# Joining two experts' rows and the attention projection: where the second expert's rows are added

## The reference

```python
x = L0_attn_x
xn = _layernorm(x, axis=-1)
x = x + _L0_attn_ref(xn, Wq, Wk, Wv, Wo, bo) + _L0_ffn_ref(xn, router_logits, gating_einsum, linear, per_expert_scale, router_scale)
```

## Time and profile before

| | |
|---|---|
| median of three runs | 814.1 us |
| the profiled execution's own time | 815.55 us |
| its span, first to last instruction | 813.8 us |
| TensorE busy in the span | 94% |
| VectorE, ScalarE, GpSimd busy | 67%, 57%, 53% |
| mean rate of all transfers | 121 GB/s |
| last scatter landed | 781.55 us |
| from there to the end of the span | 32.3 us |

### The profile page before, as it was taken

One profiled execution on the slowest core, in us unless ns is written; L12 is line 12 of the kernel. 1 busy time (PEld: TensorE's weight loads), 2 busy tenths in 40 slices (PEclk: granted clock), 3 DMA queues, 4 the chain that ended last, 5 costly groups with the idle time before them and its releaser, 6 DMA issues.

```text
span 813.8 us, 17685 instructions
## 1 busy us (share of the span) xinstructions
PE 766.9 (94%) x6172; PEld 468.4 (58%) x6172; DVE 546.2 (67%) x1419; ACT 466.9 (57%) x984; POOL 433.7 (53%) x561
## 2 busy tenths in 40 slices
PE   8999999999999999999999999879899899998997
PEld 6555554444444434444444444328889789888976
DVE  5458879999999888888888888303344334433348
ACT  3564567777777677777777777774333333333310
POOL 7665542231324545655475453264686667666676
PEclk9999999999999999999999999999999999999999
DMA  8895562513233134243442350113533333322777
GB/s 202 250 296 175 171 190 57 157 34 91 81 93 99 40 96 131 61 103 106 107 98 66 95 158 16 36 41 88 155 104 111 111 105 111 104 84 83 235 247 240
DMA packets 74912, 98.20 MB, mean 121 GB/s; under 512 B 16588, under 2 KB 54092, under 8 KB 74764
## 3 DMA queue, kind: packets, MB, share of 16 engines
q1 hardware_dynamic: 65960, 78.34, 34.2%
q0 software_dynamic: 8864, 18.72, 7.4%
HBM read 63.53 MB, written 30.75 MB: 116 GB/s over the span
## 4 chain that ended last, share of the span: by engine, by line
PE 50%; POOL 13%; issue 12%; ACT 4%; DVE 3%; DMA 2%; another core or an unknown queue 1%; DVEq 0%; POOLq 0%; ACTq 0%
PE banks L1154 17%; PE banks L754 16%; PE banks L746 13%; POOL expert_rows L1243 7%; POOL stacks L593 5%; ACT probs L1092 4%; PE banks L1339 3%; DVE stacks L1438 2%; PE banks L1348 1%; DMA stacks<-xn_rows,places 1%; DVE junk L708 1%; PE banks L1269 0%; DMA w_gu<-expert_rows 0%; DMA expert_rows<-stacks,places 0%
## 5 line engine op out<-in xcount | busy, mean ns | idle before, releaser
L708 DVE CUSTOM_DVE_ANT_0 junk<-banks,mask 128x128 bf16<-128x128 f32 (+7 forms) x512 | 359.6, 753 | 55.7 <-issue 50.6
L1092 ACT ACTIVATE probs<-banks 128x512 f32<-128x512 f32 x576 | 310.7, 606 | 102.7 <-PE banks L754 98.4
L754 PE MATMUL banks<-stacks 105*128 105x512 bf16 (+3 forms) x768 | 199.4, 329 | 10.1 <-issue 5.4
L746 PE MATMUL banks<-stacks 102*128 102x512 bf16 (+3 forms) x768 | 172.6, 326 | 2.2 <-DVE maxima L708 2.0
L885 POOL TENSOR_SCALAR_AFFINE_SELECT probs<-probs 128x512 f32<-128x512 f32 x128 | 79.9, 643 | 103.3 <-ACT probs L1092 99.5
L1321 DVE TENSOR_TENSOR probs<-banks,probs 128x256 f32<-128x256 f32 x71 | 30.1, 423 | 150.6 <-ACT probs L1285 125.0
L754 PEld LDWEIGHTS banks<-stacks 105*128 105x128 bf16 x768 | 65.6, 97 | 103.5 <-ACT probs L1092 40.5
L1154 PE MATMUL banks<-probs,ctxT 128*17 128x256 f32 (+2 forms) x1920 | 114.4, 360 | 2.0 <-DVE banks L1073 1.1
L1243 POOL DMA_INDIRECT expert_rows<-stacks,places x71 | 79.9, 1126 | 62.4 <-ACT stacks L1290 48.1
L746 PEld LDWEIGHTS banks<-stacks 102*128 102x128 bf16 x768 | 69.1, 98 | 72.2 <-DVE maxima L708 17.5
L1285 ACT ACTIVATE probs<-banks 128x256 f32<-128x256 f32 x71 | 27.3, 385 | 109.7 <-PE banks L1339 66.4
(11 more groups left out here) (129 smaller groups left out, 781.2 us busy)
## 6 DMA issues: line engine op xcount, KB each, us to landing
stacks<-qk_parts SPq DMA_DIRECT2D x192, 128.0 KB, 3.1
qk_parts<-ctxT SPq DMA_DIRECT2D x32, 384.0 KB, 3.3
xn_rows<-probs SPq DMA_DIRECT2D x8, 512.0 KB, 5.1
ctxT<-inverse_sums SPq DMA_DIRECT2D x8, 512.0 KB
w_gu<-in_w_gu SPq DMA_DIRECT2D x8, 512.0 KB
stacks<-in_x SPq DMA_DIRECT2D x16, 256.0 KB
ctxT<-expert_rows SPq DMA_DIRECT2D x16, 256.0 KB, 3.6
w_gu<-expert_rows SPq DMA_DIRECT2D x16, 256.0 KB, 5.5
```

Of the source, the lines that this page charges most:

```text
L708: last = dve.tensor_tensor_reduce(junk[:, n % RING, c:c + w], mpsum[:, slot, c:c + w], keep["mask"][:, S - w:S], 1.0, 3 * NEG, ALU.add, AL ...
L746: last = pe.matmul(mpsum[:, slot, at + c:at + e], qs[hq][0:R_MAX, h, qt * P:(qt + 1) * P], ks[hq][0:R_MAX, h, c:e], start=True, stop=True)
L754: last = pe.matmul(score_bank(("S", n, h))[:, c:c + w], ks[hq][:, h, kt * P:(kt + 1) * P], qs[hq][:, h, q0:q0 + w], start=True, stop=True)
L1092: act.activation(probs[:, u % PRING, h], score_bank(("S", n, h)), ACT.Exp, scale=SCALE).then_inc(exp_done, 1)
```

## The change

The second expert's rows are no longer loaded into a buffer of their own. GpSimd issues, for each pair, a transfer from `expert_rows` whose destination is the buffer that holds the first expert's rows of that pair, with addition as the way of writing (`accum_op`): the DMA engines read the destination, add, and write it back. GpSimd's 16 additions and the buffer in `w_gu` are gone, so are SyncE's 16 loads and its two waits ahead of them. VectorE still makes two additions for a pair: the sum of the two experts' rows to the accumulator, and the product to it. The wait on `bias_set` goes from GpSimd's queue to VectorE's.

```diff
-    done_w = Room(keep["w_gu"][:, :, :].rearrange("p e h -> p (e h)"))
     halves = [Room(keep["ctxT"][:, 2 * m + 1]) for m in range(NP // 2)]
-    yk = [[halves[n // 2]([P, 2, D]) for n in range(NP)], [done_w([P, 2, D]) for _ in range(NP)]]
+    yk = [halves[n // 2]([P, 2, D]) for n in range(NP)]
...
-            load(0, n)
-        sp.wait_ge(before["y_free"], RR + NST)
-        sp.wait_ge(before["w_ready"], NST)
-        for n in range(NP):
-            load(1, n)
+            load(n)
...
     def on_gpsimd(pool):
-        pool.wait_ge(before["bias_set"], NP)
         for n in range(NP):
             pool.wait_ge(loaded[0][n], 16)
-            pool.tensor_tensor(flat(acc[:, 2 * n:2 * n + 2, :]), flat(acc[:, 2 * n:2 * n + 2, :]), flat(yk[0][n]), ALU.add).then_inc(first_ready, 1)
+            pool.dma_start(yk[n], y_rows[1][:, 2 * n:2 * n + 2, :], accum_op=ALU.add).then_inc(loaded[1][n], 16)
...
     def on_vector(dve):
+        dve.wait_ge(before["bias_set"], NP)
         for n in range(NP):
             rows = acc[:, 2 * n:2 * n + 2, :]
-            dve.wait_ge(first_ready, n + 1)
             dve.wait_ge(loaded[1][n], 16)
-            dve.tensor_tensor(flat(rows), flat(rows), flat(yk[1][n]), ALU.add).then_inc(second_ready, 1)
+            dve.tensor_tensor(flat(rows), flat(rows), flat(yk[n]), ALU.add).then_inc(second_ready, 1)
```

More of the change, by code:

```diff
@@ L1381, in combine @@
     out_done = sem("out_done")
-    proj_ready, first_ready, second_ready, pair_done = (sem(name) for name in ("proj_ready", "first_ready", "second_ready", "pair_done"))
+    proj_ready, second_ready, pair_done = (sem(name) for name in ("proj_ready", "second_ready", "pair_done"))
     flat = lambda a: a.rearrange("p t d -> p (t d)")
@@ L1387, in on_sync, with load @@
     def on_sync(sp):
-        def load(k, n):
-            sp.dma_start(yk[k][n], y_rows[k][:, 2 * n:2 * n + 2, :]).then_inc(loaded[k][n], 16)
+        def load(n):
+            sp.dma_start(yk[n], y_rows[0][:, 2 * n:2 * n + 2, :]).then_inc(loaded[0][n], 16)
         sp.wait_ge(before["scaled"], NP)
```

## The result

| | before | changed |
|---|---|---|
| median, same chip | 814.5 us (812.2 to 816.3, 6 runs) | 821.4 us (817.8 to 824.9, 6 runs) |
| ratio | | 1.0087, interval 1.0053 to 1.0121 |
| the profiled execution, and its span | 815.55, 813.8 us | 817.79, 815.9 us |
| issue behind the last scatter's landing | 781.61 | 776.92 |
| from there to the end of the span | 32.2 us | 39.0 us |

What follows compares the result with a forecast made beforehand. VectorE set the pace before; after the change, full DMA engines: from 782.9, 16 x 1.44 + 14 x 0.72 = 33.1 us, then 0.8, 1.4 and 2.57 give 820.8, plus 0.3: 821.1 us. Range 819 to 823; 8 in 10, 810.5 to 829.

Steps and rivals of the forecast that it cites:

- The bound: After the last scatter: full DMA engines, 1.44 us per adding transfer, 0.72 per store; VectorE and TensorE wait; chance 0.38.
- The sum: Last stage: movement of 33.1 us from 782.9, then 0.8, 1.4 and 2.57 us, ending the span at 820.8.
- First landing: GpSimd's first adding transfer, issued at 781.8, lands at about 784.5 to 785.2, at load speed.
- the rival in which TensorE decides: Last stage: second read free, 0.72 us a pair, TensorE's chain sets the end; 810.4 to 811.1; chance 0.23.
- the limit of 1.66 us a pair: Spacing of adding transfers' landings at which gain turns to loss; forecast wrong if they come closer together.
- What is removed: GpSimd's 16 additions, worth at most 5.9 us through VectorE; SyncE's 16 loads and the `bias_set` wait, worth nothing.
- 3.0 to 3.7 us: Most of the 5.9 us that can be had, since TensorE's pair 4 waits for VectorE's pair 0.
- Issue: GpSimd's queue: adding transfers issued 1.3 us apart, hidden by the 1.44 us of movement.
- The rival of 2.3 us a transfer: GpSimd's issue priced per row, transfers 2.3 us apart; time 824.1 us; chance 0.12.
- The free second read: DMA engines: destination read costs nothing, 0.72 us a pair, TensorE decides; 810.4 to 811.1; chance 0.23.
- A price by piece above the double: DMA engines: adding 1 KB rows costs more than double; at three times 832.6 us; chance 0.15.
- The half price: DMA engines: second read costs half, 1.08 us an adding transfer; time 815.4 us; chance 0.12.

Runs made afterwards that it cites:

- e_plain: Changed kernel with GpSimd's 16 transfers overwriting instead of adding; stretch 29.1 us, 0.9971 against the kernel before.
- e_late_stores: Changed kernel with SyncE's 16 stores begun only when all adding transfers have landed; stretch 40.2 us, 1.0102 against the kernel before.
- v_split4: Kernel before, with VectorE making the first-row additions of pairs 0 to 9 early, four matmul banks; stretch 28.7 us, ratio 0.9991.
- e_2k: Changed kernel with each adding transfer reading 128 runs of 2 KB instead of 256 of 1 KB; stretch 36.9 us, 1.0073 against the kernel before.
- e_half: Changed kernel with only even pairs by adding transfer, odd pairs loaded by SyncE and added by VectorE; stretch 35.3 us, 1.0075 against the kernel before.

## Why the prediction was right

The time was forecast as 821.1 us, and slower; the median is 821.4. That these agree to 0.3 us is more than the prediction can claim: the changed kernel's own runs lie 7 us apart. Nor is the step from span to time sound. It added 0.3 us, the median less the span of another execution, where an execution's own time is 815.55 - 813.8 = 1.75 us above its span before and 1.9 after; the forecast span of 820.8 stands against spans of 815.9 to 823.0 with a median of 819.5. What can be held to the prediction are its steps.

- **The bound.** Forecast, with a chance of 0.38: the DMA engines are full and everything waits for the landing of adding transfers, which cost them two moves each. Shown: e_plain takes the addition away and gives back 10 us of 39; e_late_stores measures 1.36 us by itself, where 1.44 had been taken, against 0.72 to 0.77 for a plain transfer in as many packets. The pace was 2.20 us against the 2.16 of the sum. That it is the second read that costs, and not another part of adding, was argued and is not shown.
- **The sum.** From the landing to the end 820.8 - 781.55 = 39.25 us were forecast; the two traces have 39.6 and 40.0. It came out so with terms that were off in opposite ways. The DMA engines began at about 778.9, 2.6 us behind the landing, where 782.9 - 781.55 = 1.35 had been taken. Their movement lasted until about 811.1, so 32.2 us instead of 33.1. By then all 16 adding transfers were through (4.19 MB in queue 0 from 778 on), but only some 11 stores (2.92 MB in queue 1) and not 14. So the movement of each was dearer than taken: with 0.77 for a store, 16 adding transfers have 32.2 - 8.5 = 23.7 us, an estimate of 1.48 each where 1.44 was taken. The remaining 4.8 us, landing, two additions and the last store, came as forecast.
- **First landing.** 2.7 to 3.4 us after the issue were taken, from plain transfers; it was 4.7 and 4.4. This is no term of the sum above, only of the rival in which TensorE decides and of the limit of 1.66 us a pair.
- **What is removed.** VectorE's addition fell from 1.03 to 0.69, as said, and was hidden behind the waits. TensorE was said to be hidden too, and was: its last matmuls of 96 ended at 783.20 + 23.82 = 807.0, ahead of VectorE's last pairs. That 3.0 to 3.7 us were to be had with four banks is borne out by v_split4, whose stretch is 3.5 us shorter.
- **Issue.** This step was wrong, with no effect on the time. 1.3 us a transfer was taken from indirect transfers. The adding ones were begun 0.73 us apart; each kept GpSimd for 1.35 us at the least, the later ones for up to 8.9, and 16 took 19.8 us. The rival of 2.3 us a transfer is refuted by that pace: the last one was begun 10.9 us after the first, not 35. But that the number of pieces doesn't count is wrong as well: the shortest of each kind took 1.35 us with 272 packets, 1.00 with 144 (e_2k) and 0.73 with 80 (e_plain).
- **The rivals.** The free second read, 810.4 to 811.1, is what e_plain comes near: its 29.7 us from the landing with 0.3 and the 781.55 of the first trace would be 811.6. A price by piece above the double is refuted by e_2k, but for 0.14 us. The half price would be 1.08 us and 243 GB/s for adding transfers alone; measured are 1.36 and 193.

The rate from 788 to 800 was said to fall to about 250 GB/s with the share still at 1: it was 235 with 1.18.

## What to carry to other kernels

An addition that a transfer makes is not free: here it cost the DMA engines about as much as a second transfer, and it pays only where they have that much room in the very stretch where it runs. Before giving work to them, sum their moves over that stretch, stores included, and hold it against the pace of the engine that is relieved. And look first for idle time of the relieved engine just ahead: here VectorE waited 7 to 8 us before the stage, enough for ten of the 16 additions that the change wanted to be rid of (6.1 us); all 16 took 9.7.

## What the runs showed of the hardware

- An adding transfer of 256 rows of 1 KB, issued by GpSimd: 1.36 us of the full DMA engines (193 GB/s with the bytes counted once; a store 0.77 us, 341 GB/s), first landing 4.4 to 4.7 us after issue (3.1 for the same without addition), GpSimd busy for 1.35 us at the least (0.73).
- The same transfer without addition makes larger packets. Queue 0 in the section on DMA queues of the page (packets, MB, share), first of the changed kernel, then of the one without the addition: 3072 packets fewer for the same bytes, 192 for each of the 16. In the kernel before, the queue has 8864 packets without them, so an adding transfer is 272 packets and a plain one 80.

```profile
q0 software_dynamic: 13216, 22.92, 10.7%
```

```profile
q0 software_dynamic: 10144, 22.92, 8.9%
```

- Where adding transfers (queue 0) and stores (queue 1) shared the full DMA engines, the two queues moved about as many packets as each other in 12 us, whatever their size: 1479 and 1482 in the changed kernel from 796 to 808, both in pieces of 1 KB, and 1005 and 987 in e_2k from 804 to 816, where the adding ones had pieces of 2 KB and got 1.83 MB against 0.95. In the changed kernel the stores also follow the pairs one by one, so only e_2k tells this from plain lockstep.
- Beside VectorE's additions of two operands in SBUF, GpSimd's last two indirect transfers took 1.27 and 1.50 us, in six traces of six, and 0.97 in the seven traces without such additions. VectorE's additions were 0.69 us beside GpSimd's adding transfers. Beside GpSimd's own additions they are 1.03.
- TensorE had waited 3.2 us for VectorE's first pair in the changed kernel (idle from 780.0 to 783.2); from 783 to 788 its granted clock was 0.50, the lower of its two levels (1.2 GHz), and the 96 matmuls took 23.82 us instead of 20.99. Here it was hidden. In e_half, after 6.7 us of waiting, it was on the chain.
